# A ring of twelve weight places instead of eight, a folded last slab in the shared expert, and one GpSimd subtraction moved, in an attention and mixture-of-experts block on one core

## The reference

```python
x = x + attention(layernorm(x), q_kernel, k_kernel, v_kernel, out_kernel)
h = layernorm(x)
gu = h @ se_gate_up_w.T                                   # 2 x 704 features
shared = (silu(gu[:, :704]) * gu[:, 704:]) @ se_down_w.T * sigmoid(h @ shared_gate_w.T)
weights, sel = top_k(softmax(h @ gate_w.T), 4)            # of 60 experts
for e in range(60):
    gu_e = h @ w13[e].T                                   # 2 x 176 features
    sparse += cw[e][:, None] * ((silu(gu_e[:, :176]) * gu_e[:, 176:]) @ w2[e].T)
x = x + shared + sparse
```

## Time and profile before

| | before |
|---|---|
| median of 3 runs | 740.02 us (733.32 to 741.34) |
| the profiled execution | 737.07 us, of which 735.3 us is the span |
| mean granted clock of PE | 0.970 |
| attention (to about 328 us) | PE 99.88 of 100 us busy between 100 and 200 us |
| shared expert (to about 462 us) | PE 39.52 of 40 us busy between 420 and 460 us |
| routed experts (to about 722 us) | PE 41.36 of 50 us busy between 600 and 650 us |
| busy over the span | PE 678.1, ACT 502.0, DVE 438.7, POOL 320.2 us |
| DMA | 75.91 MB, 103 GB/s over the span |

### The profile page before, as it was taken

How to read it: one execution, slowest core, us unless ns; L and a number is a source line. 1 busy time by engine, 2 the same in 40 slices (tenths; PEclk the granted TensorE clock), 3 DMA queues, 4 the chain that set the end, 5 groups by cost and what they waited for, 6 DMA issues and landing times.

```text
span 735.3 us, 18110 instructions
## 1 busy us (share of the span) xinstructions
PE 678.1 (92%) x5691; PEld 357.2 (49%) x5691; DVE 438.7 (60%) x1215; ACT 502.0 (68%) x847; POOL 320.2 (44%) x400
## 2 busy tenths in 40 slices
PE   8789999999999999998899999899997978988996
PEld 6623333434434343436687887444443433444542
DVE  6864543556634464526778535667775755656758
ACT  3687878788898888872223223588886876886981
POOL 4652434244222265336204545456554553554333
PEclk9999999999999999999879999999998998999998
DMA  6000000000022000029201222177775866776686
GB/s 188 2 1 1 1 1 1 1 1 30 30 53 96 30 30 1 30 62 222 40 30 4 73 66 80 52 222 223 229 226 162 249 201 173 221 201 195 195 296 209
DMA packets 43022, 75.91 MB, mean 103 GB/s; under 512 B 7944, under 2 KB 23756, under 8 KB 42932
## 3 DMA queue, kind: packets, MB, share of 16 engines
q1 hardware_dynamic: 33556, 53.81, 24.8%
q0 software_dynamic: 9376, 20.97, 9.7%
HBM read 58.07 MB, written 16.67 MB: 102 GB/s over the span
## 4 chain that ended last, share of the span: by engine, by line
PE 75%; DVE 13%; issue 5%; another core or an unknown queue 1%; DVEq 1%; DMA 1%; SPq 1%; ACT 1%; ACTq 0%
PE p_o L1930 17%; PE p_gu L2108 13%; PE p_s L1918 11%; PE p_y L2131 8%; PE p_xs L2092 2%; PE p_hT L2118 2%; PE bench L1849 2%; PE p_d L2032 2%; PE bench L1836 2%; PE p_d L2034 1%; PE p_d L2033 1%; PE bench L1944 1%; PE bench L1966 1%; PE bench L1982 1%
## 5 line engine op out<-in xcount | busy, mean ns | idle before, releaser
L1069 ACT ACTIVATE probs<-p_s 128x1024 f32<-128x1024 f32 x256 | 243.6, 1034 | 46.4 <-PE p_s L1918 44.8
L974 ACT ACTIVATE placed<-ring 88x512 f32 x237 | 138.9, 626 | 13.7 <-PE p_d L2034 9.1
L1694 DVE COPY placed<-ring 128x704 f32 x237 | 120.1, 534 | 47.0 <-issue 24.9
L1930 PE MATMUL p_o<-probs,vext 128*32 128x512 f32 x1024 | 137.0, 608 | 0.5 <-DVE enr L1319 0.5
L949 POOL DMA_INDIRECT expert_out<-ys,goes_to x79 | 84.4, 1068 | 77.3 <-ACT ys L974 46.4
L2108 PE MATMUL p_gu<-ring,xsT 128*32 x316 | 107.0, 483 | 5.9 <-issue 5.4
L2108 PE MATMUL p_gu<-placed,xsT 128*32 128x352 f32 x948 | 107.7, 484 | 0.0
L1918 PE MATMUL p_s<-qst,kst 64*128 64x512 f32 x512 | 95.5, 449 | 3.9 <-DVE kst L1504 2.2
L920 POOL DMA_INDIRECT xs_low<-x_rows,choice_i x64 | 63.6, 994 | 69.1 <-PE p_gu L2108 32.4
L866 POOL DMA_INDIRECT members<-place,slot x48 | 47.0, 978 | 100.9 <-PE p_o L1930 83.6
L2131 PE MATMUL p_y<-placed,hT 88*32 88x256 f32 x948 | 82.7, 386 | 1.6 <-issue 1.5
(11 more groups left out here) (299 smaller groups left out, 1199.5 us busy)
## 6 DMA issues: line engine op xcount, KB each, us to landing
ring<-in_w_dram SPq DMA_DIRECT2D x60, 352.0 KB
ring<-in_w_dram SPq DMA_DIRECT2D x60, 176.0 KB
plane<-expert_out SPq DMA_DIRECT2D x10, 512.0 KB
x_rows<-rows SPq DMA_DIRECT2D x4, 520.0 KB, 3.4
x2T_kept<-xt SPq DMA_DIRECT2D x3, 512.0 KB, 2.8
x2r<-x2T_kept SPq DMA_DIRECT2D x3, 512.0 KB, 7.6
sup<-in_sup_dram SPq DMA_DIRECT2D x2, 704.0 KB, 6.2
expert_out<-ys,goes_to POOLq DMA_INDIRECT x79
```

Source lines behind the costliest of these rows:

```text
L974: return nc.scalar.activation(o, i_, ACT.Copy, **kw)
L1069: nc.scalar.activation(probs[:, j % NPB, :], p_s[j % NSB][:, :], ACT.Exp, scale=SCALE)\
L1694: last = v.tensor_copy(placed13[:, i % N13, h, :], ring[:, bass.ds(ring_at(tile, h), W13)])
L1930: last = mm(p_o[32 * g_:32 * g_ + 32, :], vext[c // 2][:, kb, rr // 2 + KP * h, :], probs[:, (2 * u + half) % NPB, h * QC:(h + 1) * QC], s ...
```

## The change

Three edits, and one row of bookkeeping.

**The ring** gets 12 places. Experts 0 to 7 keep the addresses they had (places 4 to 11); the four new places lie below, on arrays of the shared expert, and are filled when its last product is done (`sdown_in_psum`). `w13` and `w2` of an expert are loaded, freed and told apart: gate and up go six experts (`LEAD`) ahead of the way down, are freed by `gu_in_psum` and counted in `w13_arrived`, which DVE waits for; the way down's are freed by `tiles_done` and counted in `w2_arrived`, which ACT waits for. The first eight experts are loaded four at a time. `placed13`, `placed2` and `xsT` lose a slot that was not used or move, to make room.

```diff
-    RING = 8
+    RING = 12
+    EARLY = 8
+    LATE = RING - EARLY
     RELAY = 2
+    LEAD = 6
+    NSLOT = 4
...
+            def next_gate_up(e, at, before=0):
+                free_at = sp.value_load(cnt_i[0:1, 3, bass.ds(e - RING, 1)], min_val=1, max_val=NTILE + 1)
+                sp.wait_ge(gu_in_psum, free_at)
+                load_gate_up(e, at)
+                relay_gate_up(at - RELAY, before)
+
+            def next_down(e, at, before=0):
                 free_at = sp.value_load(cnt_i[0:1, 3, bass.ds(e - RING, 1)], min_val=1, max_val=NTILE + 1)
                 sp.wait_ge(tiles_done, free_at)
-                load_expert(e, s)
...
+                load_down(e, at)
+                relay_down(at - RELAY, before)
...
+                for e in range(RING, 2 * RING):
+                    next_gate_up(j * RING + (e + LEAD), e + LEAD, j * (RING // NSLOT * 16))
+                    next_down(j * RING + e, e, j * (RING // NSLOT * 16))
```

```diff
+                if f == NFS - 1:
+
+                    to, both = p_g[pair(n)][:, :], slice(2 * f * P, 2 * FS)
+                    for k in range(KC):
+                        x_high, x_low = x2h[c % 2][:, k, :], x2l[c % 2][:, k, :]
+                        mm(to, sup_h[:, k, both], x_high, start=(k == 0), stop=False)
+                        mm(to, sup_h[:, k, both], x_low, start=False, stop=False)
+                        last = mm(to, sup_l[:, k, both], x_high, start=False, stop=(k == KC - 1))
+                    last.then_inc(sgu_in_psum, 1)
+                    return
...
-                    return mm(p_d[q % 2][:, 0:C], h_low_, high, start=False, stop=(f == NFS - 1))
+                    last = mm(p_d[q % 2][:, 0:C], h_high_, low_, start=False, stop=(f == NFS - 1))
+                    if f == NFS - 1:
+
+                        return last
```

```diff
-            last.then_inc(sdown_high, 1)
+            g.tensor_copy(sdown_h[:, :, :], sdown[:, :, :]).then_inc(sdown_high, 1)
             pool.wait_ge(sdown_high, 1)
...
+            pool.wait_ge(probs_used, 3 * SPC + 8)
+            g.tensor_tensor(sdown_l[:, :, :], sdown[:, :, :], sdown_h[:, :, :].bitcast(fp32), ALU.subtract)\
+                .then_inc(sdown_split, 1)
             pool.wait_ge(x2r_loaded[0], 16)
```

More of the change, by code:

```diff
@@ L60, in attention_moe_block @@
     FS_LAST = FS - (NFS - 1) * P
+    assert 2 * FS_LAST == P
     RPC = NKV
@@ L590, in ring_at @@
         def ring_at(tile, h):
-            return ((tile >> (3 * h)) & (RING - 1)) * WE
+            return nc.s_assert_within((tile >> (4 * h)) & 15, 0, RING - 1, skip_runtime_bounds_check_because=
+                                      "a tile's word is made of places in the ring, below RING") * WE
         def wait_apart(eng, semaphore, count):
@@ L670, in _ @@
             store_rows(3)
-            for e in range(RING - RELAY):
-                relay(e, e)
+            for e in range(NSLOT, EARLY):
+                relay_gate_up(e - NSLOT)
+                load_gate_up(e, e)
+                relay_down(e - NSLOT)
+                load_down(e, e)
+            for e in range(EARLY - NSLOT, EARLY):
+                relay_gate_up(e)
+                relay_down(e)
             sp.wait_ge(tables_ready, 1)
@@ L676, in _ @@
             sp.dma_start(last_row.rearrange("o p q -> o (p q)"), last_e[:, :]).then_inc(last_loaded, 16)
-            def refill(e, s):
+            sp.wait_ge(sdown_in_psum, NT)
+            for e in range(EARLY, RING):
+                load_gate_up(e, e)
+                load_down(e, e)
+                if e >= EARLY + RELAY:
+                    relay_gate_up(e - RELAY)
+                    relay_down(e - RELAY)
+            def next_gate_up(e, at, before=0):
[3 more added lines that the diff above has]
+                relay_gate_up(at - RELAY, before)
@@ L688, in _ @@
-            NR = (E - RING) // RING
-            with sp.Fori(0, NR, 1) as j:
-                for s in range(RING):
-                    def rounds(r, slot_, j=j, s=s):
-                        return (j + (2 if s >= RELAY else 1)) * 32
-                    refill(j * RING + RING + s, s)
-            for e in range(RING * (NR + 1), E):
-                refill(e, e % RING)
-            for e in range(E - RELAY, E):
-                relay(e, e % RING)
+                load_down(e, at)
+                relay_down(at - RELAY, before)
@@ L699, in tiles_out @@
+            for e in range(E - RELAY, E):
+                relay_gate_up(e)
+            for e in range(E - LEAD, E):
+                next_down(e, e)
+            for e in range(E - RELAY, E):
+                relay_down(e)
             def tiles_out(count):
@@ L1088, in _ @@
                     act.wait_ge(sgu_in_psum, n + 1)
-                    nc.scalar.activation(sg[0:pf, pair(n), :], p_g[pair(n)][0:pf, :], ACT.Silu).then_inc(ssilu_ready, 1)
+                    nc.scalar.activation(sg[P - pf:P, pair(n), :], p_g[pair(n)][0:pf, :], ACT.Silu)\
+                        .then_inc(ssilu_ready, 1)
                 elif kind == "split":
@@ L1104, in place_down @@
                         act.wait_ge(tiles_done, i - N2 + 1)
-                    wait_apart(act, weights_arrived, tile >> (3 * PER))
+                    wait_apart(act, w2_arrived, tile >> (4 * PER))
                 for h in range(from_, to):
-                    last = copy(placed2[0:FH, i % N2, h, :], ring[0:FH, W13:][:, bass.ds(ring_at(tile, h), 2 * C)])
+                    last = copy(placed2[0:FH, i % N2, h - 1, :], ring[0:FH, W13:][:, bass.ds(ring_at(tile, h), 2 * C)])
                 if to == PER:
@@ L1557, in of_blocks @@
                 return eid[:, n * PER:(n + 1) * PER]
-            block_no, passed, real, whose, begins, inside, row_, row_or_none, slots, two, four = map(of_blocks, range(11))
+            block_no, passed, real, whose, begins, inside, row_, row_or_none, slots, two, four, rounds = map(of_blocks, range(12))
             def blocks():
@@ L1691, in place_gate_up @@
                         dve.wait_ge(gu_in_psum, i - N13 + 1)
-                    wait_apart(dve, weights_arrived, tile >> (3 * PER))
+                    wait_apart(dve, w13_arrived, tile >> (4 * PER))
                 for h in range(from_, to):
-                    last = v.tensor_copy(placed13[:, i % N13, h, :], ring[:, bass.ds(ring_at(tile, h), W13)])
+                    last = v.tensor_copy(placed13[:, i % N13, h - 1, :], ring[:, bass.ds(ring_at(tile, h), W13)])
                 if to == PER:
```

145 lines of the change are left out of this document (80 added, 65 removed).

## The result

The kernel after takes 730.9 us (median of 20 runs, 722.62 to 734.28), the kernel before 737.49 us (20 runs beside them). The ratio is 0.992, 95% interval 0.990 to 0.994: 6.6 us less, where 17 were forecast, and 730.9 lies above the range (706 to 729). The profiled execution took 732.68 us, its span is 730.9 us at a mean clock of 0.968.

What follows compares the result with a forecast made beforehand. It took PE to bound attention and the shared expert, and waits for SP's word the middle of the routed experts. 737.07 - 20.4 - 4.2 - 1.8 + 0.2 + 7.4 + 2.0 = 720.3, forecast 720 us, range 706 to 729.

Steps and rivals of the forecast that it cites:

- What bounds the kernel; why DVE waited: Routed experts: DVE waits 16.5 us for SP's word on an arrival, queued behind an unrelated load; PE waits for DVE.
- The ring, -20.4 us: Routed experts: DVE's waits for SP go and the middle 18 pairs take 5.90 us each; -20.4 us.
- The fold, -4.2 and -1.8: Shared expert: six matmuls fewer per chunk in gate and up, -4.2 us; one product fewer per way-down tile, -1.8 us.
- GpSimd's subtraction, +7.4 and +2.0: Attention: GpSimd's later operations hold DVE's Newton steps, delaying PE's turn +7.4 us; low clock behind it +2.0 us.
- Rival A: Attention: the moved GpSimd subtraction costs nothing; 711 us (703 to 714), chance 0.18.
- Rival B: Routed experts: half the ring's gain, the wait moving to ACT's copies or a load's landing; 730.5 us, chance 0.10.
- Rival C: Routed experts: SP's two rounds per expert become the bound, making it slower; 748 us, chance 0.05.
- Rival D: Routed experts: the ring isn't the cause, DVE waits as long for something else; 741 us, chance 0.02.
- The range: Whole kernel: 714 to 727 us from small terms and a ring 3 us less or 6 more; wider, 706 to 729, 0.8.
- the forecast's own case: Whole kernel: all terms hold as summed, 720 us within 714 to 727; chance 0.65.
- chance of 0.05 for a change within 1%: Whole kernel: chance 0.05 that the time lands within 1%, 7.4 us, of the kernel before.

Runs made afterwards that it cites:

- word_first: Kernel before with its eight places, SP passing on an expert's arrival before waiting for room instead of after; 689.5 us against 697.8, ratio 0.990, faster chip.
- no_reload3: `apart` without the loads of experts 12 to 59 (result of wrong weights), on a slower chip; 715.6 us, ratio 0.970.
- before_third: Kernel before, unchanged, run again for a trace on another slower chip; ratio 0.998.
- late_on_before: Kernel before with only the wait for 104 steps added ahead of GpSimd's subtraction; 743.5 us against 734.1, ratio 1.013, slower chip.
- after_again: Kernel after, unchanged, run again on a slower chip; 724.1 us, ratio 0.984.
- apart: Kernel after with GpSimd's long operations laid between DVE's chains of small operations; 713.5 us, ratio 0.968, slower chip.
- late_free: `apart` with gate and up freed by `tiles_done` instead of `gu_in_psum`; 757.4 us, ratio 1.026, slower chip.
- unfold2: `apart` with the folded slab undone; 722.8 us, ratio 0.978, slower chip.
- sub_early: Kernel after without the extra wait ahead of GpSimd's subtraction, which follows its cast at once; 683.0 us, ratio 0.981, faster chip.
- ring_alone: `sub_early` with the fold's matmuls undone, the `sdown` array and cast kept full width; 692.5 us, ratio 0.994, faster chip.
- apart2: `apart`, the same kernel, run on the faster chip; 676.9 us, ratio 0.970.

## Why the prediction was wrong, step by step

- **What bounds the kernel; why DVE waited.** Right. The wait of DVE for SP is gone from the profile after, and `word_first` shows the mechanism alone: nothing but the word's place in SP's queue was changed, and 8.3 us went.
- **The ring, -20.4 us. This is the term that failed**, and in its size: -9.7 in the two profiled executions, -9.4 on the faster chip. I took the pace of the nine undisturbed pairs for all 18, 106.2 us. They took 112.49: two pairs of 8.12 and 9.15 us remain, some 5 us together over the 6 us of their neighbours, in which the clock falls behind idle rows at issue. Such rows were there before too, 11.1 us of them in the stage against 13.5 after; those at 590 us had no fall behind them. So a low clock, which I put down to the waits alone, comes back without them; that the idle rows bring it down is read from their order and shown by no run. I also took the rest of the stage as unchanged, and it grew by 4.4 us (2.2, 0.6, 1.8 in its parts, less 0.2 at the end). `no_reload3` rules out the traffic of the weights for the pace; what delays PE at issue on these chips stays open.
- **Where the 4.4 us belong**, the other traces of slower chips show in part. The 1.8 of the last five pairs are not the ring's: the 27.8 us that I read before are 30.1 in `before_third` and 29.2 in `late_on_before`, with eight places. The 2.2 of the first six come again: 35.3 to 36.1 us in `after_again`, `apart`, `late_free` and `no_reload3`, 36.5 here, against 34.3 to 34.8 with eight places. But `unfold2`, with the same twelve places and without the fold, has 33.9, so they seem to go with the fold and not with the ring; that is one trace, and how the fold would do it isn't shown. And the -9.7 lies at the low end: other traces give the ring 15 to 18 us within a chip, nearer to the forecast, still short of it.
- **The fold, -4.2 and -1.8.** About right or a little small by itself (6 to 7.6 us on a slower chip, 9.4 on the faster, where the second stretch of low clock in the shared expert was also shorter, 3.4 us in `sub_early` instead of 10.2 in `ring_alone`), a little large for this pair of traces (-4.7), because PE now arrives early and waits 2.2, 1.4 and 1.0 us more. I had foreseen that for chunk 3's tables alone.
- **GpSimd's subtraction, +7.4 and +2.0.** Right in mechanism, place and size: an idle time of 7.20 us, attention +10.0, and 9.5 us for the edit by itself in `late_on_before`. The rule of the Trainium skill, "SBUF — State Buffer", section "Who interferes with whom", that a DVE or GpSimd instruction which takes the shared ports keeps them to its end, agrees with the rows in each trace here (6.05 us to the end of `sup_l`). That whoever issues first gets them can't be read from these rows: `den` starts at 265.92, before the cast at 266.15, and it is `den` that is held. The rule in my expectation of `apart`, that whatever DVE operation has its operands in SBUF alone is held, was too wide: the statistics of the norm weren't (1.40 and 0.38 us beside `sdown_l`). Rival A is refuted. What I missed is that the fold shifts the same race at the turn before (`sub_early`), so that taking the wait out does not give the 9.4 us back but about half (4.2 us are lost there instead).
- **Rival B** (ACT's word as the next thing to wait for) is what `late_free` does, at 40 us, with a release one step later. In the kernel after it doesn't appear, since the release by `gu_in_psum` is early enough, for the reason given against it. Its time, 730.5, is the one measured, and its bound for the ring, -10, is near the -9.7, both by luck: no wait for SP was left behind.
- **Rival C** (SP as the bound): not seen; SP keeps up with most pairs at 5.26 us on the faster chip. **Rival D**: refuted.
- **The range.** It gave the ring's term 3 us on the side of less, from the forecast's own case; the term's error is 11 us, and B's was the only case that reached there. The chance of 0.05 for a change within 1% was too small for a sum in which a gain read from a pace and a loss of half its size stand against each other.

## What to carry to other kernels

A queue that both loads and passes on arrivals should say what it knows before it waits for room: look at what stands ahead of the word, and who must finish for it. A stage's best pace is that of its undisturbed stretch only if nothing else disturbs the stretch in question; take the remaining idle rows there one by one before promising it. And long GpSimd operations belong where DVE has no chain of small operations in SBUF to get through, as `apart` lays them: a subtraction that is off every chain of waits cost 9.5 us by where it lay.

## What the runs showed of the hardware

- The same program took 734 to 737 us on some chips and 697.5 us on another. Attention was alike (326.0 and 325.4 us in `apart` and `apart2`, the same kernel); the routed stage took 227 to 228 us in the kernels with twelve places on the faster chip instead of 258 to 263 (`late_free` aside), with most pairs at 5.26 us, and PE's idle rows at "issue" in it came to 1.0 to 2.2 us instead of 10 to 15. What in the chip makes the difference isn't shown.
- DVE copies, `TENSOR_SCALAR` and `TENSOR_TENSOR` on 4 numbers a partition with operands in SBUF took 0.16 us alone and up to 6.06 beside a GpSimd operation, ending with it; `den` was held 4.20 us across two GpSimd casts that followed each other (`sup_h`, `sdown_h`). DVE's operations that read PSUM ran beside the same GpSimd operations in their usual 0.69 us, and the norm's statistics in SBUF in theirs.
- What DVE meets hangs on 0.2 us: with one GpSimd cast (1.46 us) in place of two (1.62 us together) and the subtraction right behind it, PE's wait was 4.63 us instead of 1.38.
